# Group layer norms from sums made on the way, both halves applied on ScalarE, and a feature map with one pass fewer

## The chip, the cores and the metric

One core of one Trainium2 chip runs the whole program. Its engines are TensorE (PE, with its weight loads as PEld), VectorE (DVE), ScalarE (ACT), GpSimd (POOL) and SyncE (SP, which issues DMAs here). Each engine works through its own instructions strictly in order and stops at every semaphore wait. The metric is the time on the device in microseconds, as the median of several runs; less is better.

## The reference, cut to what matters

```
x = x + LN(encoder(LN(x)))        # 4 layers, 16 heads, linear attention
x = x + LN(lora_mix(LN(x)))
x = x + LN(mamba(LN(x)))          # sequential scan over 512 steps, 16 states
x = x + LN(experts(LN(x)))        # top-1 of 8 experts

encoder layer:
    h = LN(x); q, k, v = h @ Wq + bq, h @ Wk + bk, h @ Wv + bv
    qp, kp = elu(q) + 1, elu(k) + 1            # the feature map
    x = x + attention(qp, kp, v) @ Wo + bo
    x = x + relu(LN(x) @ W1 + b1) @ W2 + b2
```

LN takes mean and variance over the last axis (256 wide), `(x - mu) * rsqrt(var + 1e-5)`. The input is 4 x 1024 rows of 256, fp32.

## The kernel before, in words

The encoder works on four batches b = 0 to 3 of 1024 rows. A batch is cut into four groups g0 to g3 of 256 rows; the tile `xb` of a group holds its residual stream as 128 partitions x 2 x 256, and `xh` its normalised rows (and later other things). Group by group, each layer does: norm 1, four transposes on PE into a PSUM bank, a high part `hT` (ACT) and a low part `hL` (DVE), the products for q, k and v, the feature map, attention, the projection Wo, a residual addition (L859), norm 2, the same transposes and parts, W1, ReLU on ACT (L1280), W2, a second residual addition (L866). After four layers each group has a tail: a final norm (FINAL), a norm of that (MID), the addition to the layer's input, a norm (MIX), the LoRA mixture, a norm (OUT) and another addition. A batch begins with a norm (FIRST) and an addition of the position table. A group so has 13 norms in a batch, 208 in all for the 16 groups.

Beside the encoder run eight Mamba units u = 0 to 7, two for each batch, each begun when the batch's rows are ready. A unit has 64 steps. A step is an exponential on ACT into a PSUM bank (L1398), a product on POOL (L1613), a scan on DVE (L990), a product on DVE (L1000) and an addition on POOL (L1626; in units 6 and 7 for three of four steps on PE instead, L631). There are three PSUM banks and a ring of five SBUF tiles for the steps in flight. Units 0 to 5 run beside batches 1 to 3, and units 6 and 7 after them; then come the experts.

**The group norm.** `sums` (L736 to L744) takes on DVE two `bn_stats` of 128x256, two `bn_aggr`, and two tiny instructions that write variance + eps into `rs` and minus the mean into `nm`. POOL's `apply` (L1513 to L1527) raises `rs` to the power -0.5 (L1517), multiplies `nm` by it (L1523) and then normalises the first half of `xb` into `xh` (L1526). ACT normalises the other half (L1210) as soon as `nm` is there. PE's transposes (L313) wait for both.

**The feature map.** ACT takes Relu(-k) from PSUM into `ek` (L1251), copies v, and takes Exp(-that) in place (L1258); DVE then forms max(k + 1, ek) into `kp` (L819). The queries do the same at twice the width (L1237, L1239, L807). A DVE result frees the PSUM bank.

**What sets the order.** Every program of an engine is a set of generators that yield a planned time before each piece; `weave` merges them by that time. The time is only a sort key. The tables `ENC`, `SLOW`, `BASE_*`, `UNIT`, `STEP`, `PRE`, `TAIL` and the offsets such as `XF`, `EXP`, `ADD`, `LN_POOL`, `LN_ACT` hold these keys. On each engine, what comes first by key is executed first, and a wait in it holds all behind it.

## Time and profile before

| | us |
|---|---|
| median of 3 runs | 3148.65 |
| the runs | 3143.81, 3148.65, 3150.6 |
| the profiled execution, own time | 3142.35 |
| its span, first to last instruction | 3141.0 |
| PE, DVE, POOL, ACT busy in it | 2371.0, 2150.1, 1822.6, 1430.0 |
| mean granted TensorE clock | 0.854 |

The profiled execution lies 6.3 us below the median and is itself between two of the runs. Busy time is that of each engine's own instructions; a matmul's end is modelled, so PE's is an upper view. Up to 440 us batch 0 runs alone; from 450 to 2450 us batches 1 to 3 run beside units 0 to 5; from 2520 to about 2860 us come units 6 and 7; the rest is the experts and the last norm. A row of the lines' view gives an instruction group, its count, total and mean time, and after the second bar how long its engine stood idle before it and for whom.

### The profile page before, as it was taken

To read this page: it belongs to the slowest core of one execution; us is meant where nothing else is said; L and a number is where in the kernel's file an instruction comes from. 1 tells how busy PE (TensorE), PEld (TensorE's weight loads), DVE (VectorE), ACT (ScalarE), POOL (GpSimd) and SP (SyncE) were. 2 spreads that over 40 slices of the span, in tenths; PEclk is the share of its full clock that TensorE was granted. 3 is DMA by queue.
4 is the path that set the end of the run, shared out by engine and by line. 5 is a ranking of instruction groups with operands and counts; after the bars stand their busy time and mean duration, and the time that the engine had idled before them with its cause. 6 is when DMAs were issued, how large, how long until landed. Compare 5 with 4: busy or idle time off the path is not lost. (4 is left out here: it accounts for less than half of the span.)

```text
span 3141.0 us, 38146 instructions
## 1 busy us (share of the span) xinstructions
PE 2371.0 (75%) x12052; PEld 1879.1 (60%) x12052; DVE 2150.1 (68%) x4707; ACT 1430.0 (46%) x2915; POOL 1822.6 (58%) x1986
## 2 busy tenths in 40 slices
PE   4999997798888757879797577888886666563770
PEld 3888984686777635858596447776875322223770
DVE  3444245877688777895588769885898697883224
ACT  3343434554554435555454455564544555332332
POOL 1111134586578856976298748872888475772214
PEclk7999998898989867999798878998998777666985
DMA  5334113131212222131122321312122123123324
GB/s 188 117 132 160 44 35 128 44 99 57 102 51 99 85 72 85 50 112 64 75 86 66 104 78 58 108 59 99 61 62 67 53 68 95 48 74 136 135 80 99
DMA packets 119482, 269.80 MB, mean 86 GB/s; under 512 B 8718, under 2 KB 61668, under 8 KB 109426
## 3 DMA queue, kind: packets, MB, share of 16 engines
q1 hardware_dynamic: 116210, 260.53, 25.7%
q0 software_dynamic: 3072, 6.83, 0.9%
q8 instruction: 99, 1.62, 0.2%
q14 instruction: 101, 0.83, 0.1%
HBM read 219.04 MB, written 49.85 MB: 86 GB/s over the span
## 5 line engine op out<-in xcount | busy, mean ns | idle before, releaser
L1613 POOL TENSOR_TENSOR sb_sc<-sb_bc,sb_du 128x512 f32<-128x512 f32 x512 | 660.8, 1295 | 115.3 <-PE ps L631 34.6
L1626 POOL TENSOR_TENSOR sb_ya<-sb_ya,sb_sc 128x512 f32<-128x512 f32 x416 | 541.1, 1302 | 82.9 <-DVE sb_sc L1000 82.6
L509 PE MATMUL ps<-sb_w,sb_fa 128*128 128x256 f32 x2048 | 484.4, 379 | 0.2 <-ACT sb_fa L1280 0.2
L1517 POOL TENSOR_TENSOR sb_g_rs<-sb_g_rs,sb_mhalf 128x2 f32<-128x2 f32 x208 | 152.7, 734 | 528.6 <-DVE sb_g_nm L744 528.2
L1398 ACT ACTIVATE ps<-sb_dl,sb_aneg 128x512 f32<-128x512 f32 x512 | 352.3, 690 | 109.7 <-DVE sb_sc L1000 100.8
L509 PEld LDWEIGHTS ps<-sb_w,sb_fa 128*128 128x128 f32 x2048 | 371.3, 190 | 42.8 <-issue 0.5
L990 DVE TENSOR_TENSOR_SCAN ps<-ps,sb_sc 128x512 f32<-128x512 f32 x256 | 312.6, 1221 | 56.1 <-ACT ps L1398 55.4
L1000 DVE TENSOR_TENSOR sb_sc<-ps,sb_bc 128x512 f32<-128x512 f32 x512 | 343.2, 671 | 0.0
L990 DVE TENSOR_TENSOR_SCAN ps<-ps,sb_hl,sb_sc 128x512 f32<-128x512 f32 x256 | 327.7, 1281 | 18.6 <-ACT ps L1398 18.4
L1280 ACT ACTIVATE sb_fa<-ps,sb_b1n 128x256 f32<-128x256 f32 x512 | 213.2, 468 | 275.9 <-PE ps L321 275.3
L631 PE MATMUL ps<-sb_sc,sb_pack 128*128 128x512 f32 x192 | 154.3, 931 | 100.6 <-DVE sb_sc L1000 100.5
L631 PEld LDWEIGHTS ps<-sb_sc,sb_pack 128*128 128x128 f32 x192 | 41.3, 265 | 205.7 <-DVE sb_sc L1000 202.9
L1251 ACT ACTIVATE sb_ek<-ps 128x256 f32<-128x256 f32 x128 | 48.7, 380 | 185.0 <-PE ps L403 184.5
L321 PE MATMUL ps<-sb_g0hT,sb_w 128*128 128x256 f32 x512 | 106.6, 309 | 13.8 <-issue 9.6
L321 PE MATMUL ps<-sb_g2hT,sb_w 128*128 128x256 f32 x512 | 102.6, 301 | 6.2 <-DVE sb_g2hL L799 6.2
L819 DVE SCALAR_TENSOR_TENSOR sb_kp<-ps,sb_ek 128x256 f32<-128x256 f32 x128 | 52.9, 417 | 77.3 <-ACT sb_ek L1258 77.3
L321 PE MATMUL ps<-sb_g3hT,sb_w 128*128 128x256 f32 x512 | 103.5, 302 | 1.7 <-DVE sb_g0xh L807 1.1
L1665 POOL TENSOR_TENSOR sb_e<-sb_yg,sb_e 128x2048 fp32r<-128x2048 f32 x8 | 36.7, 4584 | 111.2 <-ACT sb_e L1177 111.2
L321 PEld LDWEIGHTS ps<-sb_g0hT,sb_w 128*128 128x128 f32 x512 | 87.6, 207 | 20.2 <-issue 13.6
L321 PE MATMUL ps<-sb_g1hT,sb_w 128*128 128x256 f32 x512 | 98.8, 294 | 0.8 <-DVE sb_g1hL L799 0.8
L321 PE MATMUL ps<-sb_e,sb_eh 128*128 128x256 f32 (+1 forms) x576 | 77.4, 300 | 24.3 <-DVE sb_eh L1122 19.7
L321 PEld LDWEIGHTS ps<-sb_e,sb_eh 128*128 128x128 f32 (+1 forms) x576 | 75.7, 192 | 25.9 <-issue 21.1
(336 smaller groups left out, 6182.3 us busy)
## 6 DMA issues: line engine op xcount, KB each, us to landing
sb_bc<-b_and_c SPq DMA_DIRECT2D x128, 512.0 KB, 5.0
sb_w<-w_parts SPq DMA_DIRECT2D x16, 2048.0 KB, 8.6
sb_wq<-w_qkv_parts SPq DMA_DIRECT2D x16, 1536.0 KB
sb_w<-in_w SPq DMA_DIRECT2D x16, 1024.0 KB
sb_yg<-in_mw SPq DMA_DIRECT2D x16, 1024.0 KB, 5.4
gate_z<-sb_xin SPq DMA_DIRECT2D x32, 256.0 KB, 2.4
sb_zt<-gate_z SPq DMA_DIRECT2D x32, 256.0 KB, 4.2
sb_ya<-in_w SPq DMA_DIRECT2D x4, 1024.0 KB, 6.4
```

Source lines behind the costliest of these rows:

```text
L321: ins = pe.matmul(bank, lhs[x], rhs[y], start=(first and m == 0), stop=(last and m == 2), skip_group_check=True)
L509: ins = pe.matmul(acc[:, v * D:(v + 1) * D], fa[i % 3][:, h * 256 + v * 128:h * 256 + (v + 1) * 128], w2[:, 2 * f + h, :], start=(f == 0 a ...
L631: pe.matmul(held[c][:], C["ident"], db[m % RING], start=False, stop=(s == NS - 1), skip_group_check=True).then_inc(S("adp"), 1)
L819: v.scalar_tensor_tensor(out=kp[i % 3][:], in0=where["kv", i][:, 0:D], scalar=1.0, in1=ek[i % 2][:], op0=ALU.add, op1=ALU.max).then_inc(S( ...
L990: v.tensor_tensor_scan(da[m % 3][:], da[m % 3][:], db[m % RING], start, ALU.mult, ALU.add).then_inc(S("sc"), 1)
L1000: v.tensor_tensor(db[m % RING], da[m % 3][:], bc[:, i % 3, 1, :], ALU.mult).then_inc(S("cm"), 1)
L1251: n = own.tick(e.activation(ek[i % 2][:], bank[:, 0:D], ACT.Relu, scale=-1.0))
L1280: ins = e.activation(fa[i % 3][:, cols], where["w1", i][:, cols], ACT.Relu, bias=b1n[:, l, 2 * f + h2:2 * f + h2 + 1])
L1398: e.activation(da[m % 3][:], dl[:, c, :], ACT.Exp, scale=aneg[:, c, s:s + 1]).then_inc(S("ex"), 1)
L1517: i = own.tick(p.tensor_tensor(rs[:, 0:n], rs[:, 0:n], mhalf[:, 0:n], ALU.pow))
L1613: p.tensor_tensor(db[m % RING], bc[:, i % 3, 0, :], du[:, c, :], ALU.mult).then_inc(S("bm"), 1)
L1626: p.tensor_tensor(ya[:, c, :], ya[:, c, :], db[m % RING], ALU.add).then_inc(S("ad"), 1)
```

## The change

Three things are changed together, and the tables of keys are altered a little.

**The statistics of 160 of the 208 group norms.** All but FIRST, MID and OUT. The residual addition, on DVE, becomes two `scalar_tensor_tensor` of 128x256 with an accumulator output that gives the row sums `s1` (`add_summed`). One tiny instruction makes minus the mean (`mean`). ACT then takes Square(x - mean) of each half, with an accumulator output into `ss` (`squared`); the squares themselves land in `xh` and are thrown away. POOL adds one tiny instruction (`ss`/D + eps) ahead of the power. FIRST, MID and OUT keep `sums` on DVE.

**The application of all 208.** POOL no longer normalises a half; ACT does both, in two instructions (`apply_group`), and PE, DVE and SP wait for ACT alone.

**The feature map.** ACT takes Exp(k - 1) straight from PSUM, with a bias tile of -1, `bias=mone`; DVE forms max(min(e, 1), k). In `before` the bias for q and k carries b; in the new form it carries b + 1, by a scalar of 1.0 in the addition of the biases, so that k here is the old k + 1. ACT's second pass over the keys and over the queries is gone.

```
-                    v.tensor_tensor(xb[g][:], pair(where["wo", k]), xb[g][:], ALU.add).then_inc(S("xo"), 1)
+                    add_summed(g, pair(where["wo", k])).then_inc(S("xo"), 1)
...
+            def add_summed(g, second):
+                for t in range(2):
+                    ins = v.scalar_tensor_tensor(out=xb[g][:, t, :], in0=second[:, t, :], scalar=1.0, in1=xb[g][:, t, :],
+                                                 op0=ALU.mult, op1=ALU.add, accum_out=s1[g][:, t:t + 1])
+                return ins
+
+            def mean(g):
+                v.tensor_scalar(sm[f"g{g}"][3][:, 0:2], s1[g][:], -1.0 / D, None, ALU.mult).then_inc(S(f"lns_g{g}"), 1)
...
-                        v.scalar_tensor_tensor(out=kp[i % 3][:], in0=where["kv", i][:, 0:D], scalar=1.0, in1=ek[i % 2][:],
-                                               op0=ALU.add, op1=ALU.max).then_inc(S("ke"), 1)
+                        v.scalar_tensor_tensor(out=kp[i % 3][:], in0=ek[i % 2][:], scalar=1.0, in1=where["kv", i][:, 0:D],
+                                               op0=ALU.min, op1=ALU.max).then_inc(S("ke"), 1)
...
-                    sums(xb[g], f"g{g}", 2)
+                    mean(g)
...
+            def squared(g, j):
+                e.wait_ge(S(f"lns_g{g}"), j + 1)
+                for t in range(2):
+                    ins = e.activation(xh[g][:, t, :], xb[g][:, t, :], ACT.Square, bias=sm[f"g{g}"][3][:, t:t + 1],
+                                       accum_out=ss[g][:, t:t + 1])
+                ins.then_inc(S(f"lnq_g{g}"), 1)
+
+            def apply_group(x, g, j):
+                st, mv, rs, nm = sm[f"g{g}"]
+                e.wait_ge(S(f"lnp_g{g}"), j + 1)
+                for t in range(2):
+                    ins = e.activation(xh[g][:, t, :], x[:, t, :], ACT.Identity, bias=nm[:, t:t + 1], scale=rs[:, t:t + 1])
+                ins.then_inc(S(f"lna_g{g}"), 1)
...
-                        n = own.tick(e.activation(ek[i % 2][:], bank[:, 0:D], ACT.Relu, scale=-1.0))
+                        e.activation(ek[i % 2][:], bank[:, 0:D], ACT.Exp, bias=mone[:, 0:1])
...
+            def scales_group(g, b, pos, scale=None):
+                st, mv, rs, nm = sm[f"g{g}"]
+                if pos in (FIRST, MID, OUT):
+                    p.wait_ge(S(f"lns_g{g}"), norm(b, pos) + 1)
+                else:
+                    p.wait_ge(S(f"lnq_g{g}"), squares(b, pos))
+                    i = own.tick(p.tensor_scalar(rs[:, 0:2], ss[g][:], 1.0 / D, EPS, ALU.mult, ALU.add))
+                    p.wait_ge(S("pool"), i)
+                i = own.tick(p.tensor_tensor(rs[:, 0:2], rs[:, 0:2], mhalf[:, 0:2], ALU.pow))
+                p.wait_ge(S("pool"), i)
```

Of the tables, two lines show the kind: most entries move by less than 1, and of the offsets XF, ADD and EXP move most.

```
-XF = 13.33
+XF = 14.4
...
-EXP = 0.9
-ADD = 1.88
+EXP = 0.69
+ADD = 2.22
+LN_SQ = 2.18
```

The following shows one place: norm 1 of g0 ahead of the fourth layer of batch 1, where unit 1 is at its first steps. On DVE, before (L990 is a scan, L1000 its product, L866 the residual addition):

```order
L1000 TENSOR_TENSOR sb_sc<-ps5,sb_bc 128x512
L866 TENSOR_TENSOR sb_g0xb<-ps3,sb_g0xb 128x512
L738 BN_STATS sb_g0_st<-sb_g0xb 128x6 x2
L741 BN_AGGR sb_g0_mv<-sb_g0_st 128x2 x2
L743 TENSOR_SCALAR sb_g0_rs<-sb_g0_mv 128x2
L744 TENSOR_SCALAR sb_g0_nm<-sb_g0_mv 128x2
L990 SCALAR_TENSOR_TENSOR ps7<-ps7,sb_hl,sb_sc 128x512
```

The same place on DVE now (L758 is `add_summed`, L763 `mean`, L1006 the scan, L1016 its product):

```order
L1016 TENSOR_TENSOR sb_sc<-ps5,sb_bc 128x512
L758 SCALAR_TENSOR_TENSOR sb_g0xb,sb_g0_s1<-ps3,sb_g0xb 128x256 x2
L763 TENSOR_SCALAR sb_g0_nm<-sb_g0_s1 128x2
L1006 SCALAR_TENSOR_TENSOR ps7<-ps7,sb_hl,sb_sc 128x512
L1016 TENSOR_TENSOR sb_sc<-ps6,sb_bc 128x512
```

Seven norm instructions have become three; the scans around them stand where they stood.

On ACT at the same place, before (L1398 is a step's exponential, L1280 a ReLU of W1, L1210 the half norm):

```order
L1398 ACTIVATE ps7<-sb_dl,sb_aneg 128x512
L1280 ACTIVATE sb_fa1<-ps2,sb_b1n 128x256 x2
L1280 ACTIVATE sb_fa2<-ps0,sb_b1n 128x256 x2
L1398 ACTIVATE ps5<-sb_dl,sb_aneg 128x512
L1210 ACTIVATE sb_g0xh<-sb_g0xb,sb_g0_nm,sb_g0_rs 128x256
L1280 ACTIVATE sb_fa0<-ps1,sb_b1n 128x256 x2
L1398 ACTIVATE ps6<-sb_dl,sb_aneg 128x512
```

The same place on ACT now (L1433 is the exponential, L1311 the ReLU, L1232 the squares, L1240 both halves):

```order
L1433 ACTIVATE ps7<-sb_dl,sb_aneg 128x512
L1311 ACTIVATE sb_fa1<-ps2,sb_b1n 128x256 x2
L1232 ACTIVATE sb_g0xh,sb_g0_ss<-sb_g0xb,sb_g0_nm 128x256 x2
L1311 ACTIVATE sb_fa2<-ps0,sb_b1n 128x256 x2
L1433 ACTIVATE ps5<-sb_dl,sb_aneg 128x512
L1240 ACTIVATE sb_g0xh<-sb_g0xb,sb_g0_nm,sb_g0_rs 128x256 x2
L1311 ACTIVATE sb_fa0<-ps1,sb_b1n 128x256 x2
L1433 ACTIVATE ps6<-sb_dl,sb_aneg 128x512
```

The squares stand between two ReLUs and ahead of the exponential into ps5, so ACT now waits for DVE's mean there, and after that exponential for POOL.

On POOL, before (L1613 is a step's product, L1626 its addition):

```order
L1613 TENSOR_TENSOR sb_sc<-sb_bc,sb_du 128x512
L1517 TENSOR_TENSOR sb_g0_rs<-sb_g0_rs,sb_mhalf 128x2
L1523 TENSOR_TENSOR sb_g0_nm<-sb_g0_nm,sb_g0_rs 128x2
L1526 TENSOR_SCALAR sb_g0xh<-sb_g0xb,sb_g0_rs,sb_g0_nm 128x256
L1626 TENSOR_TENSOR sb_ya<-sb_ya,sb_sc 128x512
```

And now (L1572 is the added instruction, L1664 and L1677 the step's product and addition):

```order
L1664 TENSOR_TENSOR sb_sc<-sb_bc,sb_du 128x512
L1572 TENSOR_SCALAR sb_g0_rs<-sb_g0_ss 128x2
L1574 TENSOR_TENSOR sb_g0_rs<-sb_g0_rs,sb_mhalf 128x2
L1579 TENSOR_TENSOR sb_g0_nm<-sb_g0_nm,sb_g0_rs 128x2
L1677 TENSOR_TENSOR sb_ya<-sb_ya,sb_sc 128x512
```

POOL stands at the same point between the same two instructions of steps; what it waits for has moved from DVE to ACT. On PE and SP nothing is added or taken away; about a hundred of the 9,600 PE instructions change place with near neighbours.

## Rows read from the trace of the kernel before

**Rows 1.** Two stretches: busy us (instructions) of each engine, clock, DMA, GB/s.

```profile
60.00:440.00 380.00, 367.85 (x2314) 327.48 (x2313) 150.99 (x462) 150.73 (x328) 49.58 (x95) 0.99 0.30 109
...
1040.00:1240.00 200.00, 129.34 (x476) 87.82 (x476) 148.10 (x361) 89.83 (x176) 135.24 (x167) 0.75 0.25 78
```

**Rows 2.** That view, six step-dense stretches: two and the sum.

```profile
600.00:720.00 120.00, 106.28 (x626) 95.11 (x625) 100.99 (x200) 65.36 (x157) 100.87 (x98) 0.94 0.29 86
...
1560.00:1720.00 160.00, 138.71 (x819) 124.53 (x819) 142.75 (x262) 80.70 (x164) 145.21 (x145) 0.93 0.26 75
...
sum 880.00, PE 750.92 PEld 667.93 DVE 772.79 ACT 466.62 POOL 763.84; mean PE 125.15 PEld 111.32 DVE 128.80 ACT 77.77 POOL 127.31
```

**Rows 3.** Waits from 450 to 2450 us: us in total, times, longest.

```profile
POOL sb_g_rs L1517 <- DVE sb_g_nm L744: 163.1, 111, 17.1
...
DVE ps L990 <- ACT ps L1398: 63.0, 50, 5.4
...
PE ps L313 <- POOL sb_g3xh L1526: 39.3, 4, 17.1
...
DVE sb_kp L819 <- ACT sb_ek L1258: 36.0, 28, 5.6
```

**Rows 4.** DVE's L744 of the group norms in those six stretches, first and last.

```profile
600.00:720.00 120.00, 1.42 (x9) 0.94 0.29 86
...
2200.00:2360.00 160.00, 2.32 (x15) 0.93 0.21 60
```

**Rows 5.** Lines on DVE: out<-in, count, busy us, mean ns, idle before.

```profile
L743 DVE TENSOR_SCALAR sb_g_rs<-sb_g_mv 128x2 f32<-128x2 f32 x208 | 74.3, 357 | 7.2
L741 DVE BATCH_NORM_AGGREGATE sb_g_mv<-sb_g_st 128x2 f32<-128x6 f32 x416 | 62.2, 173 | 0.0
L819 DVE SCALAR_TENSOR_TENSOR sb_kp<-ps,sb_ek 128x256 f32<-128x256 f32 x128 | 52.9, 417 | 77.3 <-ACT sb_ek L1258 77.3
...
L744 DVE TENSOR_SCALAR sb_g_nm<-sb_g_mv 128x2 f32<-128x2 f32 x208 | 36.6, 176 | 0.0
...
L738 DVE BATCH_NORM_STATS2 sb_g_st<-sb_g0xb 128x6 f32<-128x256 f32 x88 | 33.0, 417 | 1.3 <-DMA sb_g0xb<-in_x_in 0.2
...
L859 DVE TENSOR_TENSOR sb_g0xb<-ps,sb_g0xb 128x512 f32<-128x512 f32 x16 | 10.9, 681 | 2.2 <-PE ps L464 2.2
```

**Rows 6.** Lines on ACT, the same columns.

```profile
L1258 ACT ACTIVATE sb_ek<-sb_ek 128x256 f32<-128x256 f32 x128 | 53.5, 418 | 0.1
L1251 ACT ACTIVATE sb_ek<-ps 128x256 f32<-128x256 f32 x128 | 48.7, 380 | 185.0 <-PE ps L403 184.5
...
L1177 ACT ACTIVATE sb_hl<-ps 128x1 f32<-128x1 f32 x256 | 42.1, 167 | 89.4 <-DVE sb_sc L1000 87.9
...
L1210 ACT ACTIVATE sb_g0xh<-sb_g0xb,sb_g_nm,sb_g_rs 128x256 f32<-128x256 f32 x44 | 26.3, 598 | 67.0 <-POOL sb_g_nm L1523 67.0
```

**Rows 7.** Lines on POOL, the same columns.

```profile
L1526 POOL TENSOR_SCALAR sb_g3xh<-sb_g3xb,sb_g_rs,sb_g_nm 128x256 f32<-128x256 f32 x44 | 26.7, 607 | 4.6
...
L1520 POOL TENSOR_SCALAR sb_g_rs<-sb_g_rs 128x2 f32<-128x2 f32 x16 | 4.1, 254 | 1.5
```

**Rows 8.** Timeline of one norm, batch 1: start us, us, instruction, idle.

```profile
907.70 0.67 DVE L866 TENSOR_TENSOR sb_g0xb<-ps,sb_g0xb 128x512 f32<-128x512 f32 x1
...
908.60 1.29 POOL L1613 TENSOR_TENSOR sb_sc<-sb_bc,sb_du 128x512 f32<-128x512 f32 x1
...
909.40 0.51 DVE L743 TENSOR_SCALAR sb_g_rs<-sb_g_mv 128x2 f32<-128x2 f32 x1
...
909.89 1.28 DVE L990 TENSOR_TENSOR_SCAN ps<-ps,sb_hl,sb_sc 128x512 f32<-128x512 f32 x1
...
910.06 0.71 POOL L1517 TENSOR_TENSOR sb_g_rs<-sb_g_rs,sb_mhalf 128x2 f32<-128x2 f32 x1 [0.17 <-DVE sb_g_nm L744]
...
911.09 0.67 DVE L1000 TENSOR_TENSOR sb_sc<-ps,sb_bc 128x512 f32<-128x512 f32 x1
911.15 0.56 POOL L1526 TENSOR_SCALAR sb_g0xh<-sb_g0xb,sb_g_rs,sb_g_nm 128x256 f32<-128x256 f32 x1
```

130 lines of the change are left out of this document (72 added, 58 removed).

## Prediction

> **What bounds the kernel now.** I first read the busy time by stretches, since the shares over the whole span mix stages with different limits. From 60 to 440 us, with batch 0 alone, PE is busy for 367.9 of 380 us while DVE, ACT and POOL have less than half of it [rows 1]: this stage is PE's. Its clock is granted at 0.99 there. In six stretches where Mamba steps and encoder layers run side by side, 880 us together, no engine stands out: DVE is busy for 772.8, POOL for 763.8, PE for 750.9 (88, 87 and 85%), and only ACT, with 466.6, has room [rows 2]. At a batch's end and the next one's start, as from 1040 to 1240 us, PE is busy for 129.3 of 200 and every other engine too is idle for a quarter or more [rows 1]; there chains of small steps set the pace.
>
> Next the waits. From 450 to 2450 us DVE's scans wait 63.0 us for ACT's exponentials [rows 3], and POOL is not among their large releasers; POOL on the other hand waits 163.1 us, 111 times, for DVE's mean [rows 3]. So where steps and layers mix, DVE leads and POOL follows closely. At the four ends of a batch PE waits for a normalised g3, 39.3 us in 4 waits, up to 17.1 at once [rows 3]. That is the chain-bound place.
>
> **DVE's part.** One layer norm with its residual addition costs now 681 (addition) + 2 x 417 + 2 x 173 + 357 + 176 = 2394 ns [rows 5]. Afterwards it is two additions of 128x256, nearest to the feature map's 417 ns of the same operation, shape and kind of source, and one tiny instruction in the place of L743, 357 ns [rows 5]. The trace has no accumulator output. Its price lies between nothing, since bn_stats too reduces 256 columns for 417, and a small DVE instruction, bn_aggr's 173 [rows 5]. I take the upper end, because a small instruction is the nearest row to a separate write of one column. So 2 x (417 + 173) + 357 = 1537 ns: DVE saves 857 ns a norm, 1203 if the accumulator is free.
>
> The Trainium skill, "VectorE: DVE Perf Modes", section on two Vector instructions with no wait between them, says that an operation that writes out its accumulator is two instructions, the second a read of the accumulator. No run here shows it yet; by it the upper end would stand.
>
> The tiny instruction is less certain than its mean. In the timeline of one norm L743 took 0.51 us and ended when POOL's product, 1.29 us long from 908.60, had ended (909.89) [rows 8], whereas the average of all is 357 and its successor L744, which follows at once, 176 [rows 5]. The new mean comes earlier, and may be held for up to a POOL instruction. Priced at 0.36 it costs what L743 costs; held for most of 1.29 each time, DVE would save nothing.
>
> The Trainium skill, "SBUF — State Buffer", section on its two separate sides, says that GpSimd and those DVE instructions that use both ports lock out each other for a whole instruction. The 0.51 us agrees with it. By the rule a shorter DVE norm meets the same locks and gives part of the 857 ns back; by the mean row it keeps it.
>
> **POOL's part.** It loses the application, 607 ns in g3, and gains one tiny instruction, 254 [rows 7]: 0.33 us less a norm, on all layer norms. What it is waiting for comes from ACT instead of DVE.
>
> **ACT's part.** An application with two pointers takes 598, an SBUF pass without one 418 [rows 6], so a pointer costs 90. A square with one is 508, with an accumulator read of 0 to 167 (a one-column ACT copy [rows 6]) 508 to 675; at the upper end, two are 1.35 us. The second application adds 0.60. So +1.95 us a norm. Against it each key tile loses a pass of 418 and its first pass pays 90 more (a bias pointer): -0.33 us, 128 times; the queries do the same at double width 64 times. ACT's sum grows by about 250 us in 3141 and stays the least busy of the four.
>
> **The chain of one norm**, from the start of the residual addition to the rows in `xh`, now runs from 907.70 to 911.71: 4.0 us [rows 8]. Of its pieces DVE's shrink by 857 ns; the two squares add 1350 and POOL's instruction 254; two applications of 598 in a row stand for one of 607 beside one of 598, 589 more. -857 + 1350 + 254 + 589 = 1336: **1.3 us longer**, with one hand-over more, and 0.7 if both accumulators are free. In the stage of batch 0 PE has other groups' products queued between the norm and its transposes, and DVE and ACT are idle for more than half; I cost the longer chain there at nothing. Without that cover it would be 32 layer norms x 1.3 = 42 us. FIRST, MID and OUT change only in the application: one instruction on each of two engines at once becomes two in a row, +0.6 us.
>
> **The sum.** In the six dense stretches L744 counts 9, 12, 8, 15, 9 and 15 group norms, 68 (the first and the last are shown) [rows 4]. DVE's load falls there from 772.8 by 68 x 0.86 = 58 to 715, POOL's from 763.8 by 68 x 0.33 = 22 to 742. The fuller of the two falls from 773 to 742: I take those **31 us**, and no more, since POOL becomes the bound before DVE's saving is used up. In the other stretches of batches 1 to 3 neither engine is near full, and I take nothing. Keys: DVE's L819 waits 28 times for the pass that goes (36.0 us [rows 3]), and 0.33 less on half of them is **4 us**. At the four batch ends g3 goes through FINAL, MID, MIX, OUT, and the next batch through FIRST and its first norm 1: three norms of the long kind at 1.3 and three at 0.6, 5.7 us an end and 23 for four. PE's waits of up to 17.1 us there show the chain exposed, but steps of a unit run beside it, so I take **14 us** (range 5 to 25). 31 + 4 - 14 = 21 less: 3142.35 - 21 = 3121 for the profiled execution. That execution lies 6.3 below the median of the runs, so as a median 3148.65 - 21 = **3128**.
>
> **Rival 1, slower: ACT in order.** ACT now has two waits in each norm, for the mean and for the scale, with step exponentials queued behind them, for which DVE's scans wait. At the place shown ahead, one exponential stands between squares and application. From the mean on, DVE has about two steps, scan and product, before it needs the exponential behind the application: 2 x (1.28 + 0.67) = 3.9 us [rows 8]. ACT needs the squares (1.35), POOL's three instructions (0.25 + 0.71 + 0.2, the last one taken at the 0.2 between the power's end and the application's start), the application (1.2) and the exponential (about the two-pointer 0.6): 4.3 us, and a ReLU may stand in between. So 0.4 to 0.8 us of wait could be added to DVE in each norm, and it decides once ACT comes later than those 3.9 us. In the 68 dense norms that is up to 54 us; three quarters of it, with the chain's 14 and less the 35 saved, gives +20: **3169**. Against it: today's wait for exponentials is 63.0 us in 2000 [rows 3], although ACT already waits for POOL once in each norm.
>
> The Trainium skill, "ScalarE: Activation LUTs", rules for kernel authors, speaks against moving elementwise work to ScalarE, since VectorE is faster for each element. In rows, DVE's 417 against about 508 and ACT's 598 for the same 256 columns agree; by it the total of engine work grows, and only ACT's room pays for it.
>
> **Rival 2: the whole DVE saving counts.** If POOL, freed of 0.33 us and of waiting on L744, keeps up, 68 x 0.86 to 1.2 is 58 to 82; with 70, the keys and the chain that is 3149 - 70 - 4 + 14 = **3089**. For it speaks that POOL mostly waits for DVE, against it that POOL is 87% busy.
>
> **Rival 3: nothing moves.** PE is busy for 85% of the dense stretches, not far from its 97% with batch 0 alone; a faster DVE may only let the steps run ahead of layers that PE then sets, and the chain takes the rest: **3149**.
>
> **Chances.** The forecast's kind (7 to 40 us less) 0.40, rival 2 (more than 40 less) 0.14, rival 3 (within 6 us) 0.17, rival 1 0.29. A measurement of this kernel tells about 0.2%, 6.3 us, from no change: faster 0.54, same 0.17, slower 0.29. The range for 8 in 10 reaches into both sides: 3086 to 3178.
>
> **What would show it.** Right: the dense stretches' load of DVE falls by about 60 us of 773 and the same scans are done in less time; the two additions take 0.42 to 0.58 us each; batch 0 ends within 3 us of where it did; the batch ends grow by 1 to 6 us each. Wrong: DVE's scans wait for L1398's successor by well over 63 us (rival 1); POOL's waits ahead of its power grow beyond 163 us; or an accumulator output costs more than a small instruction, which makes the squares and additions each dearer and the chain longer.

## The result, and the profile after

The changed kernel takes 3152.49 us (median of 20 runs, 3142.15 to 3160.44), the kernel before in the same comparison 3147.91 us (20 runs, 3140.26 to 3152.61). The ratio is 1.0019, with a 95% interval of 1.0010 to 1.0028: some 6 us slower by the ratio, 4.6 by the two medians. A gain of 21 us was forecast; the time lies in the range but not on the side of the forecast. The profiled execution took 3153.72 us, its span is 3152.1; the profiled execution before had 3142.35 and 3141.0, so this pair is 11 us apart, more than the kernels are.

First the busy time of the engines over the whole span, from the page of the changed kernel.

```profile
PE 2387.1 (76%) x12052; PEld 1889.5 (60%) x12052; DVE 1996.9 (63%) x4387; ACT 1613.1 (51%) x3567; POOL 1724.9 (55%) x1939
```

DVE lost 153 us of its 2150.1, POOL 98 of its 1822.6, and ACT gained 183. So the work moved as planned, and yet the span grew. Next the view of [rows 1], of the changed kernel: batch 0 alone, and a batch's end. Columns are PE, PEld, DVE, ACT and POOL busy, then clock, DMA share and GB/s.

```profile
60.00:440.00 380.00, 366.77 (x2299) 326.89 (x2298) 121.79 (x396) 175.21 (x426) 35.86 (x92) 0.99 0.30 109
1040.00:1240.00 200.00, 123.55 (x453) 82.04 (x451) 138.47 (x347) 110.02 (x233) 119.34 (x154) 0.74 0.25 78
```

Batch 0 is PE's as before. In the stretch at the batch's end PE does 123.6 us of work in 200 instead of 129.3. The same view in the six stretches of [rows 2], two of them and the sum:

```profile
600.00:720.00 120.00, 102.92 (x621) 92.75 (x622) 96.73 (x192) 70.48 (x181) 98.45 (x96) 0.95 0.26 81
...
1560.00:1720.00 160.00, 133.45 (x804) 119.97 (x804) 135.28 (x242) 97.66 (x222) 140.15 (x142) 0.94 0.24 72
...
sum 880.00, PE 744.48 PEld 663.60 DVE 717.81 ACT 532.72 POOL 731.84; mean PE 124.08 PEld 110.60 DVE 119.64 ACT 88.79 POOL 121.97
```

DVE's load fell from 772.8 to 717.8 and POOL's from 763.8 to 731.8, very near the 715 and 742 of the forecast. PE, which does the layers' work there, did 744.5 us of it instead of 750.9.

These stretches are fixed in time, and the changed kernel comes to them late: in batch 1, g0's FINAL is applied at 1032.73 us, 8 us later than before:

```profile
1024.58 0.60 ACT L1210 ACTIVATE sb_g0xh<-sb_g0xb,sb_g_nm,sb_g_rs 128x256 f32<-128x256 f32 x1 [1.12 <-POOL sb_g_nm L1523]
```

So I also measured between marks that move with the work, the starts of ACT's applications. The layers of batches 1 to 3, each from g3's first norm 1 to g0's FINAL, took 1394.4 us together before and 1378.1 in the changed kernel, **16 us less**. The four batch ends, each from g0's FINAL to g3's first norm 1 of the next batch (the last one to the end of the span), took 1317.1 and 1339.8 us, **23 us more**. Batch 0 gives the other 5 us: its first norm 1 of g3 is applied 2.7 us later, and its layers take 2.1 us more. These sums are from one execution of each kernel.

Now the waits from 450 to 2450 us, as [rows 3] has them (us, times, longest):

```profile
DVE ps L1006 <- ACT ps L1433: 145.1, 112, 5.0
...
POOL sb_g_rs L1572 <- ACT sb_g3xh L1232: 64.2, 19, 11.1
POOL sb_g_rs L1574 <- DVE sb_g_nm L750: 54.4, 27, 6.6
...
PE ps L319 <- ACT sb_g3xh L1240: 43.1, 6, 15.4
...
DVE sb_kp L835 <- ACT sb_vx L1193: 42.4, 27, 6.9
```

Before, PE waited for ACT's half of g3 too:

```profile
PE ps L313 <- ACT sb_g3xh L1210: 10.0, 3, 7.7
```

DVE's scans wait 145.1 us for the exponentials, up from 63.0, and POOL, which waited for DVE's mean, now waits for ACT's squares as well (those in g3 are shown, 64.2 of 192.8 in all four groups). With POOL's 54.4 us for DVE's mean that makes 247.2 us of wait ahead of the power, where 163.1 stood. PE's waits for normalised rows of g3 fell from 49.3 (39.3 for POOL's half, 10.0 for ACT's) to 43.1; over all four groups they rose from 73.5 to 87.8. The key's step waits 42.4 us, where 36.0 stood. Last the lines, with the columns of [rows 5]: DVE, then ACT, then POOL.

```profile
L763 DVE TENSOR_SCALAR sb_g_nm<-sb_g_s 128x2 f32<-128x2 f32 x160 | 67.0, 420 | 4.3
...
L758 DVE SCALAR_TENSOR_TENSOR sb_g0xb<-ps,sb_g0xb 128x256 f32<-128x256 f32 x64 | 24.4, 418 | 11.9 <-PE ps L515 9.7 <-PE ps L470 2.2
...
L758 DVE SCALAR_TENSOR_TENSOR sb_g2xb<-sb_g2xh,sb_g2xb 128x256 f32<-128x256 f32 x16 | 10.2, 669 | 11.4 <-DMA sb_g2xb<-in_pe 11.3
...
L758 DVE DVE_READ_ACCUMULATOR sb_g0xb<-ps,sb_g0xb 128x1 f32 x64 | 5.3, 82 | 0.0
```

```profile
L1284 ACT ACTIVATE sb_ek<-ps,sb_mone 128x256 f32<-128x256 f32 x128 | 60.5, 473 | 189.0 <-PE ps L409 188.4
...
L1232 ACT ACTIVATE sb_g0xh<-sb_g0xb,sb_g_nm 128x256 f32<-128x256 f32 x80 | 39.9, 502 | 24.1 <-DVE sb_g_nm L763 24.0
...
L1232 ACT ACTIVATION_READ_ACCUMULATOR sb_g0xh<-sb_g0xb,sb_g_nm 128x1 f32 x80 | 15.3, 191 | 0.0
```

```profile
L1572 POOL TENSOR_SCALAR sb_g_rs<-sb_g_ss 128x2 f32<-128x2 f32 x160 | 32.8, 205 | 562.3 <-ACT sb_g0xh L1232 221.2 <-ACT sb_g3xh L1232 133.3 <-ACT sb_g1xh L1232 104.1
```

An accumulator output shows as a second instruction: 82 ns on DVE, 191 on ACT, beside the 418 and 502 of the main one. The addition with both inputs in SBUF took between 669 ns (g2) and 514 ns (g3) on average, the same with one input in PSUM 418.

### The profile page after: what moved, and what is told of

Same layout as the page of the kernel before. It is cut to its first block and busy times, and to the rows that moved or that the text cites. A ratio compares the mean times of both kernels' runs of the same rounds, so it can differ in the third digit from the quotient of the medians.

```text
span 3152.1 us, 38370 instructions
## 1 busy us (share of the span) xinstructions
PE 2387.1 (76%) x12052; PEld 1889.5 (60%) x12052; DVE 1996.9 (63%) x4387; ACT 1613.1 (51%) x3567; POOL 1724.9 (55%) x1939
## 5 line engine op out<-in xcount | busy, mean ns | idle before, releaser
L1664 POOL TENSOR_TENSOR sb_sc<-sb_bc,sb_du 128x512 f32<-128x512 f32 x512 | 661.6, 1296 | 129.9 <-PE ps L637 36.9
L1677 POOL TENSOR_TENSOR sb_ya<-sb_ya,sb_sc 128x512 f32<-128x512 f32 x416 | 534.7, 1286 | 65.1 <-DVE sb_sc L1016 64.9
L1433 ACT ACTIVATE ps<-sb_dl,sb_aneg 128x512 f32<-128x512 f32 x512 | 352.2, 689 | 88.7 <-DVE sb_sc L1016 77.1
L1006 DVE TENSOR_TENSOR_SCAN ps<-ps,sb_sc 128x512 f32<-128x512 f32 x256 | 313.4, 1225 | 103.7 <-ACT ps L1433 102.2
L1006 DVE TENSOR_TENSOR_SCAN ps<-ps,sb_hl,sb_sc 128x512 f32<-128x512 f32 x256 | 328.3, 1283 | 60.2 <-ACT ps L1433 60.1
L1016 DVE TENSOR_TENSOR sb_sc<-ps,sb_bc 128x512 f32<-128x512 f32 x512 | 343.5, 672 | 0.0
L1572 POOL TENSOR_SCALAR sb_g_rs<-sb_g_ss 128x2 f32<-128x2 f32 x160 | 32.8, 205 | 562.3 <-ACT sb_g0xh L1232 221.2
L1311 ACT ACTIVATE sb_fa<-ps,sb_b1n 128x256 f32<-128x256 f32 x512 | 212.1, 466 | 182.5 <-PE ps L327 181.6
L1284 ACT ACTIVATE sb_ek<-ps,sb_mone 128x256 f32<-128x256 f32 x128 | 60.5, 473 | 189.0 <-PE ps L409 188.4
L835 DVE SCALAR_TENSOR_TENSOR sb_kp<-sb_ek,ps 128x256 f32<-128x256 f32 x128 | 52.7, 415 | 90.4 <-ACT sb_vx L1193 90.3
```

Of the source, the lines that this page charges most:

```text
L835: v.scalar_tensor_tensor(out=kp[i % 3][:], in0=ek[i % 2][:], scalar=1.0, in1=where["kv", i][:, 0:D], op0=ALU.min, op1=ALU.max).then_inc(S( ...
L1006: v.tensor_tensor_scan(da[m % 3][:], da[m % 3][:], db[m % RING], start, ALU.mult, ALU.add).then_inc(S("sc"), 1)
L1016: v.tensor_tensor(db[m % RING], da[m % 3][:], bc[:, i % 3, 1, :], ALU.mult).then_inc(S("cm"), 1)
L1284: e.activation(ek[i % 2][:], bank[:, 0:D], ACT.Exp, bias=mone[:, 0:1])
L1311: ins = e.activation(fa[i % 3][:, cols], where["w1", i][:, cols], ACT.Relu, bias=b1n[:, l, 2 * f + h2:2 * f + h2 + 1])
L1433: e.activation(da[m % 3][:], dl[:, c, :], ACT.Exp, scale=aneg[:, c, s:s + 1]).then_inc(S("ex"), 1)
```

## The experiments

Every kernel was timed in five rounds against the kernel before, on the same chip. "Ratio" is to the kernel before; 0.001 is 3.1 us. A difference of two of these ratios has itself an error, of 5 to 7 us by their intervals; where it matters it is given. Together they give this ladder:

| kernel | ratio | 95% interval |
|---|---|---|
| before with feature map alone | 0.9962 | 0.9950 to 0.9975 |
| before with both applications on ACT alone | 0.9948 | 0.9935 to 0.9961 |
| both of these, old sums, old tables | 0.9908 | 0.9895 to 0.9921 |
| the same with the new tables | 0.9917 | 0.9901 to 0.9932 |
| and new sums in the seven layer norms | 0.9911 | 0.9897 to 0.9925 |
| and new sums at the first norm 1 too | 0.9929 | 0.9916 to 0.9943 |
| and new sums at FINAL and MIX: the change | 1.0019 | 1.0010 to 1.0028 |

### The parts one by one

**The feature map alone.** In the kernel before, ACT's two passes become one, with the bias row one higher:

```
- n = own.tick(e.activation(ek[i % 2][:], bank[:, 0:D], ACT.Relu, scale=-1.0))
+ e.activation(ek[i % 2][:], bank[:, 0:D], ACT.Exp, bias=mone[:, 0:1])
...
- e.activation(ek[i % 2][:], ek[i % 2][:], ACT.Exp, scale=-1.0).then_inc(S("kx"), 1)
```

> The kernel before with the shorter feature map alone: one exponential from PSUM in the place of a ReLU and an exponential, the bias row one higher, the key's readiness given by the value copy. Norms and tables as before. Theory A (the new kernel's loss is the norms', not this part's): a gain by what the prediction gave it, about 4 us, ratio 0.998 to 1.000, and the key's step on DVE waits less than before's 77 us over the whole run. Rival B (this part costs, since the key now waits for the copy behind the exponential): ratio 1.001 or more, and the same wait at 77 us or above.

Measured: 0.9962, 12 us less. The key's wait on DVE, 36.0 us in [rows 3], became, in the same view:

```profile
DVE sb_kp L821 <- ACT sb_vx L1179: 26.7, 22, 4.1
```

Theory A holds for this part, and it gains three times the 4 us forecast; 9 us of it show in this wait. (Between the two profiled executions the difference is only 3.8 us, 3141.0 to 3137.2, so single executions are no measure of such a size.)

**Both applications on ACT, nothing else.**

```
-                    apply(xb[g], f"g{g}", xh[g], norm(b, pos(l)), (1,))
+                    apply_group(xb[g], g, norm(b, pos(l)))
```

`apply` did half 1 on ACT; `apply_group` does both, and POOL's `scales_group` ends with the product that makes `nm`.

> The kernel before with one thing changed: ACT applies both halves of every group norm, POOL none; statistics, feature map and tables as before. Theory A: ACT later by 0.6 us a norm, half of what squares and application add together, partly paid by POOL's 0.6 less: ratio 1.000 to 1.005, and the scans' wait for exponentials rises from before's 74 us towards 110. Rival D (POOL's load was what mattered): ratio 0.993 to 0.998.

Measured: 0.9948, 16 us less. POOL's busy time fell from 1822.6 to 1700.8 us, ACT's rose from 1430.0 to 1526.3, and DVE's scans waited 59.3 us for exponentials, not more than the 63.0 of before. So an ACT that is later by 0.6 us a norm does not hold up the scans here, and the move is a gain. POOL's wait for DVE's mean grew meanwhile from 163.1 to 207.8 us, in a kernel that is faster.

**The two together, the base of all that follows.**

> The kernel before with two parts together: the shorter feature map, and both applications of every group norm on ACT; statistics (bn_stats and bn_aggr on DVE) and tables as before. If the two parts add up as measured one by one (0.9962 and 0.9948): ratio 0.991, about 28 us less. If they draw on the same slack: 0.994 to 0.996. What is then between this kernel and the changed one is the new statistics with their tables, +1.1% or +0.7%.

Measured: 0.9908. The parts add up (28 us one by one, 29 together). This kernel is faster than both kernels of the study, and it has none of the new sums: the new sums with their tables cost 1.1%.

**The application shared again, in the changed kernel.**

```
-                for t in range(2):
+                for t in (1,):
```

That is ACT's loop in `apply_group`; half 0 goes back to POOL, behind L1579.

> The changed kernel, statistics as changed (row sums from the additions, squares on ACT), but every application shared again: first half on POOL, second on ACT. Theory A (ACT in order: squares and two applications hold up the step exponentials): ACT gives back 0.59 us a norm, DVE's scans wait for exponentials clearly less than the 162 us of the changed kernel (under 130), ratio against before 0.995 to 1.000. Theory C (the chain of a norm at the batches' ends): chain 0.6 us shorter in each of the 13 norms, 6 of them at a batch's end, so some 3 us for each of four, ratio about 0.998. Rival D (POOL bound): POOL gets 0.61 us a norm back, and the time stays or rises, ratio 1.002 to 1.006.

Measured: 1.0054, interval 1.0039 to 1.0068: slower still. ACT was busy for 1512.7 us instead of 1613.1, and yet its wait row in the view of [rows 3] reads:

```profile
DVE ps L1006 <- ACT ps L1433: 160.5, 107, 5.9
```

That is more than the changed kernel's 145.1, with 100 us less of work on ACT. Theories A and C both fall in the form in which they stood; D's number came.

**The old tables in the changed kernel.**

> The changed kernel with the tables of planned times of the kernel before (the one new entry, for the squares, kept). Theory A (what costs is the work on ACT, and the new tables help a little against it): ratio against before 1.002 to 1.010. Rival E (the new tables themselves cost, exponentials 0.2 us and the second addition 1.07 us later): ratio at or under 1.000.

Measured: 1.0043, interval 1.0029 to 1.0057. The new tables are worth 0.24% to the changed kernel, and nothing to the one with old sums (0.9917 with them, 0.9908 without).

### Where the new sums cost

**Old sums at the batch ends alone, and the counterpart.** A tuple of positions says where the new form is used; elsewhere the addition is one instruction again, `sums` runs on DVE and ACT takes no squares:

```
+        NEW = (2, 3, 4, 5, 6, 7, 8)      # the counterpart: (1, 9, 11)
+                if pos not in NEW:
+                    return v.tensor_tensor(xb[g][:], second, xb[g][:], ALU.add)
...
+                if pos not in NEW:
+                    return sums(xb[g], f"g{g}", 2)
```

> The changed kernel with the old statistics (one addition, bn_stats, bn_aggr on DVE, no squares) at the batch ends alone: the first norm of layer 0, FINAL and MIX; the seven other layer norms keep the new form. Theory C (the longer chain at the batch ends costs, 3 norms x 1.3 us x 4 ends = 16 us): ratio against before 0.996 to 0.998. Theory F or G (the loss sits in the dense stretches): ratio stays at 1.000 to 1.003.

> The counterpart: the new statistics at the batch ends alone, the old ones in the seven other layer norms of each batch and group (the tables of the changed kernel). Theory C: ratio against before 0.998 to 1.002, since the chain's cost stays. Theory F or G: 0.991 to 0.996, as the applications and the feature map give it, and the scans' wait for exponentials falls to before's 63 us from 450 to 2450.

Measured: 0.9911 with the new sums in the layers alone, 1.0007 (0.9998 to 1.0015) with them at the ends alone. So 48 of the 160 norms carry the whole loss: 0.0108 or 34 us (error 5) when they are taken back from the changed kernel, 0.0090 or 28 us (error 6) when they are added to the kernel with old sums and new tables (0.9917). The prediction had 14 us for all that changes at the ends. And the wait for exponentials, in the first of these two:

```profile
DVE ps L1011 <- ACT ps L1441: 129.4, 108, 4.8
```

129.4 us of wait in a kernel that is 34 us faster than the changed one with 145.1. With the old sums in the layers too (0.9917) the same wait is 84.6 us, and the time is the same within the error. The row that looked like the proof of rival 1 is not where the time went.

**FINAL and MIX alone old.**

> The changed kernel with the old statistics in FINAL and MIX alone (2 of the 3 kinds at a batch end); the first norm of layer 0 keeps the new ones. All three old gave 0.9911. If FINAL and MIX, which come in a row for each group, carry the loss: 0.991 to 0.994. If each of the three kinds carries a third: 0.995. If the first norm of layer 0 does: 0.998 or more.

Measured: 0.9929. FINAL and MIX carry 0.0090, 28 us (error 5); the first norm 1 carries 0.0018, 6 us, which is no more than its error.

**Short squares.** To see whether it is their length, the squares read 16 columns instead of 256, with every wait kept:

```
-                    ins = e.activation(xh[g][:, t, :], xb[g][:, t, :], ACT.Square, ...)
+                    ins = e.activation(xh[g][:, t, 0:16], xb[g][:, t, 0:16], ACT.Square, ...)
```

> The changed kernel with squares over 16 of the 256 columns (the variance is taken from these 16): every wait and every instruction stays, only the time of the two squares falls, from about 0.5 us each to about 0.25. Theory F (the squares' time on ACT is what costs): ratio against before 0.990 to 0.996 and the scans' wait for exponentials well under 145 us from 450 to 2450. Theory G (the additional hand-over costs, DVE's mean to ACT to POOL, in which ACT stands and holds up what is queued): no more than a third of the loss comes back, ratio 0.998 to 1.002, and the scans' wait stays over 110 us.

> The changed kernel with squares over 16 columns at the first norm of layer 0, FINAL and MIX alone (variance from these 16); in the layers they are whole. Short squares everywhere measured 0.9910. Theory C (the chain at the ends costs): most of that comes back, ratio 0.991 to 0.995. Theory F (ACT's time in the layers): ratio 0.999 to 1.002.

> The counterpart: short squares in the seven other layer norms, whole ones at the ends. Theory C: ratio 0.999 to 1.002. Theory F: 0.991 to 0.995.

The short square's row (columns as in [rows 6]):

```profile
L1232 ACT ACTIVATE sb_g0xh<-sb_g0xb,sb_g_nm 128x16 f32<-128x16 f32 x80 | 23.8, 301 | 24.7 <-DVE sb_g_nm L763 24.4
```

301 ns instead of 502, so 0.40 us less in each norm. The variance is then that of 16 columns, so these kernels serve only to measure time. Short everywhere: 0.9910, 34 us less than the changed kernel. At the ends alone (48 norms, 19 us of squares): 0.9969, 16 us less (error 6), 0.8 for each us (0.5 to 1.1). In the layers alone (112 norms, 45 us): 0.9964, 17 us less (error 5), 0.4 for each us (0.3 to 0.5). Neither theory has it all: length counts at both, and more at the ends. Theory G falls, since waits and hand-overs were kept; of theory F the ratio came, but not the fall of the scans' wait (138.9 us with short squares everywhere, 145.1 in the changed kernel).

**Doubled squares at the ends.**

```
+                if j % 13 in (1, 9, 11):
+                    for t in range(2):
+                        n = own.tick(e.activation(xh[g][:, t, :], xb[g][:, t, :], ACT.Square, ...))
+                    e.wait_ge(S("act"), n)
```

> The changed kernel with each square done twice at the first norm of layer 0, FINAL and MIX: 1.4 us more in each of 48 norms (12 at each of four batch ends), 67 us in all. If all four groups' norms stand in one row at an end, as the 16 us from 0.4 us less in each let one think (0.8 for each us): about 55 us more, ratio 1.017 to 1.022. If only one group's chain counts, as the prediction had it: 3 norms x 1.4 x 4 = 17 us more, 1.006 to 1.008.

Measured: 1.0158, interval 1.0141 to 1.0174, a little under the first range, so 0.0139 or 44 us more (error 6) for 67: 0.65 for each us. One group's chain alone would have given 17. More than one group's norms count at an end.

**How that row looks.** At the end of batch 1, ACT's application of FINAL in g0 opens it and the one of MIX in g3 closes it. Timeline rows (start, us, instruction, idle time before): the changed kernel, then the one with the new sums in the layers alone, then the doubled squares, with its MIX of g3 as well. For the first two, MIX of g3 stands in the views further down (1124.54 and 1112.42).

```profile
1032.73 1.09 ACT L1240 ACTIVATE sb_g0xh<-sb_g0xb,sb_g_nm,sb_g_rs 128x256 f32<-128x256 f32 x2 [1.23 <-POOL sb_g_nm L1579]
```

```profile
1025.41 1.10 ACT L1245 ACTIVATE sb_g0xh<-sb_g0xb,sb_g_nm,sb_g_rs 128x256 f32<-128x256 f32 x2 [1.06 <-POOL sb_g_nm L1587]
```

```profile
1045.35 1.09 ACT L1245 ACTIVATE sb_g0xh<-sb_g0xb,sb_g_nm,sb_g_rs 128x256 f32<-128x256 f32 x2 [0.65 <-POOL sb_g_nm L1584]
...
1143.71 1.09 ACT L1245 ACTIVATE sb_g3xh<-sb_g3xb,sb_g_nm,sb_g_rs 128x256 f32<-128x256 f32 x2 [1.37 <-POOL sb_g_nm L1584]
```

From start to start that is 91.8 us in the changed kernel, 87.0 with the old sums at the ends and 98.4 with doubled squares. Over the four ends it is 343.9, 323.9 and 377.5: **20 us of the 34 arise inside these four rows**, which hold 8 norms of the long kind each. With FINAL and MIX alone old they take 323.3 us, so the 20 us are those two norms'. Of the rest, 9.7 lie between the rows (the first norm 1 is there), 6.1 behind the last one, and -1.6 ahead of the first. The doubled squares put 8 x 4 x 1.4 = 45 us into the rows, and these grew by 33.6, which is all of the 33.7 us between the two profiled executions (the medians are further apart). In the rows PE is busy for 227 of the 344 us.

The kernels with the old sums everywhere do not fit this count as well: their rows take 335.8 us (new tables) and 336.6 (old tables), 12 more than with the new sums in the layers alone, though by their ratios these kernels are equally fast. So the sums' effects in the layers and at the ends do not simply add up; why is open.

And one norm in it, MIX of g3 at that place. The changed kernel:

```profile
1119.99 0.42 DVE L758 SCALAR_TENSOR_TENSOR sb_g3xb<-sb_g3xh,sb_g3xb 128x256 f32<-128x256 f32 x1 [0.21 <-ACT sb_g3xh L1240]
1120.14 1.40 POOL L1664 TENSOR_TENSOR sb_sc<-sb_bc,sb_du 128x512 f32<-128x512 f32 x1
...
1120.35 1.47 DVE L758 SCALAR_TENSOR_TENSOR sb_g3xb<-sb_g3xh,sb_g3xb 128x256 f32<-128x256 f32 x1
...
1121.86 0.17 DVE L763 TENSOR_SCALAR sb_g_nm<-sb_g_s 128x2 f32<-128x2 f32 x1
...
1122.07 0.51 ACT L1232 ACTIVATE sb_g3xh<-sb_g3xb,sb_g_nm 128x256 f32<-128x256 f32 x1 [1.53 <-DVE sb_g_nm L763]
...
1122.57 0.49 ACT L1232 ACTIVATE sb_g3xh<-sb_g3xb,sb_g_nm 128x256 f32<-128x256 f32 x1
...
1123.25 0.19 POOL L1572 TENSOR_SCALAR sb_g_rs<-sb_g_ss 128x2 f32<-128x2 f32 x1 [1.70 <-ACT sb_g3xh L1232]
1123.52 0.71 POOL L1574 TENSOR_TENSOR sb_g_rs<-sb_g_rs,sb_mhalf 128x2 f32<-128x2 f32 x1
...
1124.54 1.09 ACT L1240 ACTIVATE sb_g3xh<-sb_g3xb,sb_g_nm,sb_g_rs 128x256 f32<-128x256 f32 x2 [1.38 <-POOL sb_g_nm L1579]
...
1125.77 0.45 PE L319 MATMUL ps<-sb_pack,sb_g3xh 128*128 128x128 f32 x1 [14.89 <-ACT sb_g3xh L1240]
```

The one with old sums at the ends:

```profile
1109.36 0.69 DVE L759 TENSOR_TENSOR sb_g3xb<-sb_g3xh,sb_g3xb 128x512 f32<-128x512 f32 x1 [0.20 <-ACT sb_g3xh L1245]
1109.50 1.67 POOL L1672 TENSOR_TENSOR sb_sc<-sb_bc,sb_du 128x512 f32<-128x512 f32 x1
...
1110.09 0.75 DVE L745 BATCH_NORM_STATS2 sb_g_st<-sb_g3xb 128x6 f32<-128x256 f32 x2
...
1111.17 0.16 DVE L751 TENSOR_SCALAR sb_g_nm<-sb_g_mv 128x2 f32<-128x2 f32 x1
...
1111.41 0.71 POOL L1582 TENSOR_TENSOR sb_g_rs<-sb_g_rs,sb_mhalf 128x2 f32<-128x2 f32 x1 [0.23 <-DVE sb_g_nm L751]
...
1112.42 1.09 ACT L1245 ACTIVATE sb_g3xh<-sb_g3xb,sb_g_nm,sb_g_rs 128x256 f32<-128x256 f32 x2 [2.51 <-POOL sb_g_nm L1587]
...
1113.66 0.66 PE L320 MATMUL ps<-sb_pack,sb_g3xh 128*128 128x128 f32 x2 [14.13 <-ACT sb_g3xh L1245]
```

From the addition's start to PE's transposes it took 5.78 us with the new sums and 4.30 with the old. PE has been idle for 14 us in both when it begins: nothing of PE's covers the chain here. Where nothing is in the way, as at the same norm of batch 0, the two forms take 4.71 us (497.22 to 501.93) and 4.28 (498.08 to 502.36), only 0.43 apart: DVE's shorter part nearly pays for the squares and for POOL's added instruction. At the place shown the difference is 1.48, and 1.05 of it is the second addition. It took 1.47 us where it takes 0.42 alone, and it ended at 1121.82, 0.28 us behind the end of POOL's product (1121.54). The old addition, in one instruction, began before POOL's product and took its 0.69; POOL's product was the one that took longer (1.67).

The Trainium skill, "SBUF — State Buffer", section on its two separate sides, says that a DVE instruction with two inputs in SBUF and a GpSimd instruction that reads SBUF exclude each other, and that who starts first holds the pair of ports for its whole instruction. The two timelines agree: both additions read two SBUF tiles, and here cutting one in two gave POOL a gap to step into. The additions from PSUM, in the layers, stay at 416 to 419 ns.

The cut is not the only way into such a wait, though. In the kernel before, the undivided addition of MIX meets it as well, as at g0 of the same batch end, where POOL's product starts just ahead of it:

```profile
1033.08 1.29 POOL L1613 TENSOR_TENSOR sb_sc<-sb_bc,sb_du 128x512 f32<-128x512 f32 x1
...
1033.18 1.74 DVE L895 TENSOR_TENSOR sb_g0xb<-sb_g0xb,sb_g0xh 128x512 f32<-128x512 f32 x1 [0.43 <-POOL sb_g0xh L1526]
```

Over a whole execution these waits make the SBUF additions of MIX and of the first norm 1 longer by 8 us in the kernel before, by 3 once both applications are on ACT, by 2 with the new sums in the layers alone, and by 11 in the changed kernel, in each case almost only in the twelve MIX norms that have units beside them. So the new sums brought back what the applications' move had taken away, with 0.7 to 2.0 us in nine of the twelve norms.

### What the layers give

**Is DVE's time worth anything there?**

> Feature map and both applications on ACT with the old statistics everywhere, as in the kernel that measured 0.9908, but with the changed kernel's tables. It differs from the kernel with the new sums in the layers (0.9911) by those sums alone. If the new sums in the layers gain what the prediction gave them (DVE and POOL lighter, 31 us): this one has 1.000 or more. If they gain nothing (theory H: ACT's squares and the hand-over take back what DVE saves): 0.990 to 0.992. Between: 0.993 to 0.997.

Measured: 0.9917 against 0.9911. The new sums in 112 layer norms are worth 2 us, with an error of 7: nothing that can be told from zero, and not 31. The marks say the same: the layers of batches 1 to 3 take 1371.7 us with the old sums (1367.0 with the old tables) and 1374.5 with the new ones, so the changed kernel's 16 us of gain there are not the sums'. In the six dense stretches the kernel with the old sums has DVE busy for 776.5 us, no less than the kernel before (772.8), and by the ratio it is 26 us faster.

**DVE's time taken away, nothing else.** `bn_stats` reads 16 of 256 columns in these norms:

```
-                    first = own.tick(v.bn_stats(st[:, t, :], x[:, t, :])) - t
+                    first = own.tick(v.bn_stats(st[:, t, :], x[:, t, 0:w])) - t
```

> Feature map and both applications on ACT, new tables, old statistics everywhere (0.9917), but in the seven layer norms of each batch and group bn_stats reads 16 of 256 columns (mean and variance from these): about 2 x 0.25 us less of DVE a norm, 112 norms, 56 us, and the chain as much shorter, ACT and POOL as before. If DVE's time in the layers is worth what the prediction took (all of it while DVE is the fuller engine): some 25 us of these in the dense stretches, ratio 0.982 to 0.986. If it is worth nothing: 0.990 to 0.992.

```profile
L740 DVE BATCH_NORM_STATS2 sb_g_st<-sb_g2xb 128x6 f32<-128x16 f32 x56 | 7.1, 168 | 0.9
```

168 ns instead of 417, 0.50 us a norm, 56 us in all (mean and variance are then those of 16 columns). Measured: 0.9889 against 0.9917, 9 us with an error of 7: **0.16 for each us of DVE**, at most 0.3. That lies between the two ranges of the expectation; the prediction had taken each us as a whole one.

**ACT's time taken away there, with old sums at the ends.**

> Old statistics at the batch ends, new ones in the layers with squares over 16 columns (variance from these). The same with whole squares measured 0.9911; short squares in the layers of the changed kernel gave 0.55% (1.0019 to 0.9964). Theory H (in the layers ACT's time in the squares takes back what DVE saves): the 0.55% comes again, ratio 0.985 to 0.987. Theory I (DVE's and ACT's load in the layers is worth nothing as long as the ends set the pace): 0.990 to 0.992.

Measured: 0.9885 against 0.9911, 8 us (error 6) for 45: 0.18 for each us. With new sums at the ends the same step gave 17 (error 5). The two losses may well depend on each other, but 9 us with an error of 8 do not show it. Of theory H's 17 us half came; the ratio lies between the two ranges.

**One square on each engine.**

```
+                v.scalar_tensor_tensor(out=xh[g][:, 1, :], in0=xb[g][:, 1, :], scalar=nm[:, 1:2], in1=xb[g][:, 1, :],
+                                       op0=ALU.add, op1=ALU.mult, accum_out=ss[g][:, 1:2])
```

> Old statistics at the ends; in the layers one half's square on ACT, the other's on DVE at the same time (sum of (x - mean) times x with an accumulator, some 0.6 us). Against the kernel with both on ACT (0.9911): ACT 0.69 us a norm lighter, DVE 0.6 heavier, chain 0.6 shorter. Theory H: ratio 0.986 to 0.989. If DVE's time counts as much as ACT's: 0.990 to 0.993.

Measured: 0.9974, 20 us slower (error 6) than with both squares on ACT, outside both ranges. The row shows what was not expected (columns as in [rows 5], slowest and fastest group):

```profile
L771 DVE SCALAR_TENSOR_TENSOR sb_g3xh<-sb_g3xb,sb_g_nm 128x256 f32<-128x256 f32 x28 | 26.5, 946 | 1.0
...
L771 DVE SCALAR_TENSOR_TENSOR sb_g2xh<-sb_g2xb,sb_g_nm 128x256 f32<-128x256 f32 x28 | 21.8, 778 | 1.0
```

This too reads two SBUF operands. It took 0.78 to 0.95 us on average, and 0.48 to 0.49 in batch 0, where no unit runs beside it; its accumulator read adds 0.08. DVE's busy time rose by 91 us (2026.5 to 2117.2), where 67 were meant. That the longer instruction and its waits for POOL are the whole reason is not shown: at 0.16 for each us, 91 us would cost 15.

**What the applications' move to ACT gains.**

> The kernel before with both applications on ACT (0.9948), plus one instruction on POOL behind every norm's scale in the place of the application that left, over 256 columns of a constant into a tile that nothing reads: POOL's load is back, the norm's result still comes from ACT alone. If the gain of 0.5% was POOL's lighter load: ratio 0.998 to 1.001. If it was the order (results ready without POOL's queue): 0.994 to 0.996.

```profile
L1546 POOL TENSOR_SCALAR sb_spare<-sb_mhalf 128x256 uint8<-128x256 f32 x208 | 260.5, 1252 | 0.0
```

The spare instruction, from a constant to bytes, took 1.25 us instead of the application's 0.56 to 0.61, so 260 us were put on POOL, not 122. Measured: 1.0174, 71 us more than without it, 0.27 for each us, and outside both ranges, since the load put on was twice the one meant. If taking a us away is worth what adding one costs, the 122 us that POOL really lost are worth 33, more than the 16 gained, and ACT's longer application can have taken the rest. So POOL's load is enough to explain the gain; that it is the cause, or the only one, is not shown.

**Shared applications at the ends, with old sums.** `ENDS` is the six norms of a batch's end and start:

```
+                for t in (1,) if j % 13 in ENDS else (0, 1):
```

> The kernel before with the shorter feature map, old statistics and old tables; both applications on ACT in the seven layer norms alone, one half each on POOL and ACT at the six norms of a batch's end and start. Both on ACT everywhere measured 0.9908. If the row of norms at the ends counts in full: 4 groups x up to 6 norms x 0.49 us x 4 ends, at 0.8, up to 38 us less, ratio 0.979 to 0.986. If POOL's load counts there as well: 0.988 to 0.993.

Measured: 0.9926 (0.9910 to 0.9942) against 0.9908: no gain, and the 6 us of difference are within the error of 7. Each of these norms should be 0.49 us shorter (two applications of 1.09 in a row against one of 0.60), but the four rows together are as long as before (342.1 us from the first application's start to the last one's end, 340.8 with both on ACT). A part of the answer stands in the trace: with the applications shared, DVE's waits for POOL in the SBUF additions of MIX and OUT are back at 8.4 and 5.2 us (8.3 and 5.2 in the kernel before), where both on ACT had 2.6 and 4.2. The addition then starts when POOL's application ends, and POOL's next product starts at about the same time, as in the view of the kernel before above. These 7 us are less than the 24 us that the 48 norms FINAL, MID and MIX should give in the rows, so the rest stays open.

## Why the prediction was wrong, step by step

**What bounds the kernel.** That batch 0 is PE's and covers the longer chain held: its last low part ends at 456.7 us before and at 459.8 after, and nearly all of these 3.2 us were there at the first one (51.2 to 54.4). That DVE leads in the mixed stretches was read from its 88%. The rows are right, the conclusion was not: with 56 us less of DVE the kernel gains 9, and with none less it gained 26 by other parts.

**DVE's part.** The accumulator read is an instruction of its own, as the upper end had it, but costs 82 ns and not 173; the mean took 420, not 357. A norm takes 2 x (417 + 82) + 420 = 1418 ns instead of 1537. The dense stretches' load fell by 55 us (58 forecast). So this term was sized rightly.

The Trainium skill, "VectorE: DVE Perf Modes", section on two Vector instructions with no wait between them, has the second instruction; the trace agrees, with 82 ns. Of the port rule I had thought at the mean (357 ns before, 420 after), and not at the additions that read SBUF alone, to which it adds 11 us over the run (8 in the kernel before).

**POOL's and ACT's part.** The prediction put POOL's saving at 0.33 us a norm, though 607 - 254 is 0.35; this changes its 22 us to 24. POOL's load fell by 32 us. A square with its read is 502 + 191 = 693 ns in the rows, though the next instruction starts 0.09 us before the read's end; 675 was the upper end. ACT's busy time grew by 183 us, 250 forecast.

**The chain.** Forecast 1.3 us longer. Where nothing else runs, the changed kernel's MIX took 4.71 us and the old one, with the applications shared, 3.80 (492.18 to 495.98): 0.9. Where units run beside it, at the one place shown, the new sums alone made it 1.48 longer. The step is right in kind; that DVE's additions there wait for POOL's products was missing.

**The sum against the marks.** The prediction was 31 + 4 less in the layers, 14 more at the ends and nothing in batch 0: 21 less. Between the marks of the two profiled executions it came out as 16 less, 23 more and 5 more: 11 more (6 by the ratio of all runs). The layers' term missed by 19 us, the ends' by 9, batch 0's by 5.

**First failed step: "I take those 31 us".** The fuller engine's loss of load was taken as time, all of it. The load fell as forecast and the time did not. The new sums, which make DVE's part of it, gave 2 us with an error of 7 in the layers; a us of DVE taken away alone gave 0.16, one of ACT 0.18 to 0.4, and one put on POOL cost 0.27. By 0.16 and 0.18 the layers' 112 norms give 0.16 x 0.98 x 112 = 18 us for DVE and take 0.18 x 1.39 x 112 = 28 for ACT; as each price has an error of more than half its size, they only say that the two can cancel. What the layers did gain came with the applications' move and the feature map. In these stretches, with DVE, POOL and PE busy for 85 to 88%, none of them was the bound by itself.

**Second failed step: "three norms of the long kind at 1.3 and three at 0.6, 5.7 us an end ... I take 14 us".** It followed g3 alone. In the trace the four groups' FINAL and MIX stand in one row of 66 to 95 us at each end, with PE waiting in it, and the doubled squares show that eight long norms count there (33.6 us for 45), where g3 has two. The new sums alone cost 34 us at the ends (28 by the counterpart). An estimate from the traces: 48 norms at the undisturbed 0.43 us are 21 us, DVE's waits for POOL add 9 (11 against 2), and of these 30 us, at 0.65 to 0.8 for each, 19 to 24 would come out as time; the remainder is not accounted for. That all the ends together are only 23 us longer than before, inside the range of 5 to 25, is partly luck: without the new sums there the ends take 1307.6 us, 10 less than before, and this gain was not forecast.

**Keys.** 4 us forecast; 12 measured for the feature map alone (8 to 16 by its interval), of which 9 show in the key's wait. In the changed kernel the key's wait went up instead, from 36.0 to 42.4; what else on ACT delays the key there was not tried.

**The rivals.** Rival 1 gave the right sign for a mechanism that does happen (63.0 to 145.1 us) and does not carry the loss: 129.4 us of that wait stand in a kernel at 0.9911, and 160.5 in one with less ACT work. A DVE with less to do probably shows its spare time in this wait, whoever is late. The prediction's other sign, POOL's wait ahead of its power beyond 163 us, came too (247.2), and is as little a proof: it is 207.8 in a kernel that is 16 us faster. Rival 3, "nothing moves", has the number (3149 for 3152); of its reasons "the chain takes the rest" is shown, "PE sets the layers" is not. Rival 2 falls. The gain of the applications' move (16 us) had no term of its own; it was part of the 31.
